# A decoder layer with experts on one core: another order of the step, routing in PSUM, and set-up loads counted in four groups

## The reference

```
x = x + self_attention(layernorm(x))             # 16 heads of 8, rope, causal
x = x + cross_attention(layernorm(x), ctx)       # 16 heads of 8, 77 keys
xn = layernorm(x)
p = softmax(xn @ router_w)                       # 8 ways; top1 picks one
shared = (xn @ sup * silu(xn @ sgate)) @ sdown   # hidden 512
routed = expert[top1](xn)                        # 7 experts, hidden 512; way 7 has none
x = x + 2 * p[top1] * routed + shared
```

## Time and profile before

| what | value |
|---|---|
| times of three runs | 1065.08, 1065.98, 1068.63 us; median 1065.98 |
| span of the profiled execution | 1065.7 us (that execution has no other time beside it) |
| start of the batch loop's first project_qkv | 26.1 us |
| last project_qkv, last shared_down, first expert matmul | 776.6, 842.62, 856.95 us |
| PE, DVE, ACT, POOL busy over the span | 93%, 82%, 69%, 59% |
| mean granted TensorE clock | 0.990 of full |

### The profile page before, as it was taken

How to read it: one execution, slowest core, us unless ns; L and a number is a source line. 1 busy time by engine, 2 the same in 40 slices (tenths; PEclk the granted TensorE clock), 3 DMA queues, 4 the chain that set the end, 5 groups by cost and what they waited for, 6 DMA issues and landing times.

```text
span 1065.7 us, 45022 instructions
## 1 busy us (share of the span) xinstructions
PE 992.5 (93%) x16200; PEld 818.3 (77%) x16201; DVE 870.9 (82%) x2853; ACT 737.2 (69%) x1557; POOL 631.4 (59%) x1488
## 2 busy tenths in 40 slices
PE   1579999999999999999999999999999999999995
PEld 1357777777777777777777777777777889999995
DVE  4367999999999999999999999999986457777774
ACT  0267878888888878888888888887875145555552
POOL 0346677777777677777777777767764124444443
PEclk9999999999999999999999999999999899999998
DMA  6222011000100010000100010000000122222220
GB/s 133 71 72 77 28 32 32 26 30 26 32 26 30 25 29 28 26 30 26 32 26 30 26 29 28 30 25 28 28 29 21 58 70 70 73 71 68 70 65 5
DMA packets 66648, 44.27 MB, mean 42 GB/s; under 512 B 24135, under 2 KB 61451, under 8 KB 66592
## 3 DMA queue, kind: packets, MB, share of 16 engines
q1 hardware_dynamic: 55424, 30.35, 10.5%
q0 software_dynamic: 5312, 12.18, 3.3%
q10 hardware_dynamic: 5856, 0.99, 0.7%
HBM read 23.96 MB, written 18.29 MB: 40 GB/s over the span
## 4 chain that ended last, share of the span: by engine, by line
PE 76%; DVE 10%; issue 4%; SPq 3%; DMA 2%; ACT 1%; POOL 1%; ACTq 1%; DVEq 0%; POOLq 0%
PE pv L1122 11%; PE scores L1302 6%; PE scores L1307 6%; PE ro L1318 6%; PE ro L1177 6%; PE scores L1163 5%; PE st L1232 5%; DVE arena L641 4%; PE scores L999 4%; PE scores L1169 4%; PE ro L1139 3%; PE pj L1145 3%; PE ro L1131 3%; PE ro L1150 2%; PE scores L1033 2%
## 5 line engine op out<-in xcount | busy, mean ns | idle before, releaser
L919 ACT ACTIVATE arena<-scores 128x1024 f32<-128x1024 f32 (+1 forms) x256 | 262.6, 1026 | 48.5 <-PE scores L1016 33.6
L641 DVE TENSOR_REDUCE arena<-scores 128x8 f16<-128x1024 f32 (+1 forms) x256 | 256.7, 1003 | 47.5 <-PE scores L1007 37.6
L859 ACT ACTIVATE arena<-st 128x128 f16<-128x128 f16 (+2 forms) x256 | 154.9, 605 | 7.9 <-PE st L1232 6.8
L859 ACT ACTIVATE arena<-arena 128x512 f16<-128x512 f32 (+2 forms) x192 | 92.9, 484 | 70.3 <-POOL arena L453 50.3
L1122 PE MATMUL pv<-arena 128*32 128x128 f32 (+1 forms) x4096 | 139.3, 277 | 0.0
L1122 PEld LDWEIGHTS pv<-arena 128*32 128x32 f32 (+1 forms) x4096 | 104.6, 110 | 17.1 <-issue 10.1
L439 POOL TENSOR_TENSOR arena<-arena,neg_half 128x1 f32<-128x1 f32 x192 | 106.5, 555 | 15.0
L449 POOL TENSOR_TENSOR arena<-arena 128x256 f32<-128x256 f32 x64 | 46.4, 725 | 78.9 <-DVE arena L633 78.9
L526 POOL DMA_INDIRECT out_dram<-x_tile x70 | 69.9, 998 | 38.5 <-POOL carried L525 26.1
L477 POOL TENSOR_TENSOR arena<-arena 128x128 f32<-128x128 f32 x128 | 51.7, 404 | 61.2 <-DVE arena L651 61.2
L1232 PE MATMUL st<-id,arena 128*128 128x128 f16 (+1 forms) x1024 | 74.0, 215 | 8.5 <-POOL arena L462 8.5
(11 more groups left out here) (175 smaller groups left out, 2681.3 us busy)
## 6 DMA issues: line engine op xcount, KB each, us to landing
x_tile<-xs SPq DMA_DIRECT2D x70, 129.0 KB, 2.0
arena<-arena SPq DMA_DIRECT2D x512, 4.0 KB
arena<-in_x_dram SPq DMA_DIRECT2D x64, 64.0 KB, 1.8
out_dram<-pay SPq DMA_DIRECT2D x64, 64.0 KB, 1.6
arena<-in_ctx_dram SPq DMA_DIRECT2D x64, 38.5 KB
w_gate<-in_L_ffn_gate_w_dram SPq DMA_DIRECT2D x7, 256.0 KB, 2.8
w_up<-in_L_ffn_up_w_dram SPq DMA_DIRECT2D x7, 256.0 KB, 3.1
w_down<-in_L_ffn_down_w_dram SPq DMA_DIRECT2D x7, 256.0 KB, 4.0
```

Source lines behind the costliest of these rows:

```text
L641: v.tensor_reduce(nmax[:, n, :].rearrange("p (m r s) -> p r m s", r=2, s=SLOT)[:, u, :, 0:HG], pair(s)[:, :, 0:HG * keys].rearrange("p m ( ...
L859: return a.activation(to, of, ACT.Copy)
L919: a.activation(e32[0:rows, 2 * n + u, :], scores[0:rows, 1024 * s:1024 * (s + 1)], ACT.Exp).then_inc(sexp_done[n][u], 1)
```

## The change

It does six things. (1) Every engine's step gets another order and other lags: PE now from 0 (`xT1_of`) to 10 (`router`, `shared_gate`, `shared_up`, `positions`, `shared_down`), DVE 0 to 10, POOL and ACT 0 to 9. (2) The pieces are put on other banks: gate and the positions on pv, up and down on st, stacks and both `values` on ro; the two pairs of `scores` hold scores alone. (3) Routing reads its logits in PSUM and writes its marks there; `logits_copy` and the identity matmul go, and `run_of` adds the base in a double buffer `run_pos`. (4) The variance plus eps and the negated mean move from POOL to DVE; the four `carry` go. (5) The loads count four semaphores, part of them go from ACT's queue to SP's, the set-up of cross attention runs inside steps 1 and 2, and a tanh loads ACT's table early. (6) The set-up's temporaries lie in the tile buffers instead of the loop's. The expert weights are still issued from step 3 on.

```diff
-        W_SELF = 16 * 10
-        W_ALL = 16 * 23
+        W_SELF = 16 * 5
+        W_ALL = 16 * 17
...
+            act.wait_ge(setup_z, 1)
+            a.activation(tanh_s[:, 0, 0:1], empty[:, 0:1], ACT.Tanh)
...
-            def logits_copy(b, p):
-                v.tensor_copy(logits[:, p, :], ro[:, 3 * P:3 * P + E]).then_inc(logits_ready, 1)
+            def top_of(b, p):
+                wait(dve, logits_psum, b + 1)
+                v.tensor_reduce(top[:, p:p + 1], pj[:, 0:E], axis=AX.X, op=ALU.min).then_inc(top_ready, 1)
             def marks_of(b, p):
-                v.scalar_tensor_tensor(out=mark[:, :], in0=logits[:, p, :], scalar=top[:, p:p + 1], in1=marks,
+                v.scalar_tensor_tensor(out=pj[:, E:2 * E], in0=pj[:, 0:E], scalar=top[:, p:p + 1], in1=marks,
                                        op0=ALU.is_equal, op1=ALU.mult).then_inc(marked, 1)
...
             def run_of(b, p):
-                v.tensor_copy(run_base[:, :], ro[:, 2 * P + E:2 * P + 2 * E]).then_inc(run_ready, 1)
+                v.tensor_tensor(run_pos[:, p, :].rearrange("p (n e) -> p n e", n=2), run_pos[:, 1 - p, E:2 * E].unsqueeze(1).to_broadcast([P, 2, E]),
+                                pv[:, 0:2 * E].rearrange("p (n e) -> p n e", n=2), ALU.add).then_inc(run_ready, 1)
+            def hot_pos_of(b, p):
+                v.scalar_tensor_tensor(out=hot_pos[:, :], in0=run_pos[:, p, 0:E], scalar=1.0, in1=hot16[:, p, :],
...
+            def ln1_var_of(b, p):
+                v.tensor_scalar_add(varp[:, 0:1], mv[:, 0, p, 1:2], EPS).then_inc(ln_var[0], 1)
...
+            nm0_turns = (((sh_hid, -7),), ((k2_ready, -3), (val2_ready, -3),), ((q2_ready, -3),), ((sh_added, -8),), ((nmT_ready[0], 0),),)
+            def self_max_turned(b, p):
+                turn(pe, b, *nm0_turns)
...
             def step(i, p):
+                at(i, p, 10, router)
+                at(i, p, 6, project_q2)
+                at(i, p, 10, shared_gate)
+                early(i, 10, busy_gate)
+                at(i, p, 6, project_kv2)
+                late(i, 6, busy_kv2)
+                at(i, p, 7, cross_max_turned)
+                two_turns(i, p, self_max, 2, 1, 0, sm1_turns, self_exp, 3, 0, 1, se0_turns)
+                at(i, p, 8, cross_values)
+                at(i, p, 10, positions)
+                at(i, p, 1, project_qkv)
+                late(i, 1, busy_qkv)
+                two_turns(i, p, self_exp, 3, 1, 0, se1_turns, self_max, 2, 0, 1, sm0_turns)
+                at(i, p, 6, stacks2)
+                at(i, p, 5, xT2_of)
+                at(i, p, 10, shared_up)
+                at(i, p, 3, self_values)
+                at(i, p, 2, self_max_turned)
+                at(i, p, 4, project_self_out)
+                two_turns(i, p, cross_exp, 7, 1, 0, ce1_turns, cross_max, 6, 0, 1, cm0_turns)
+                at(i, p, 8, project_cross_out)
+                at(i, p, 9, xT3_of)
+                at(i, p, 5, ctxT_of)
+                at(i, p, 10, shared_down)
+                early(i, 10, busy_down)
+                at(i, p, 0, xT1_of)
+                two_turns(i, p, cross_max, 6, 1, 1, cm1_turns, cross_exp, 7, 0, 0, ce0_turns)
+                at(i, p, 1, stacks)
```

More of the change, by code:

```diff
@@ L772, in _ @@
+                at(i, p, 9, hidden_of)
+            run(dve, step, 10)
             links = [0]
@@ L1110, in two_turns, with stack4 @@
                         round2(s2, u2, p2, g)
-            def values(b, p, n, *users):
-                vals, rows = ((val, P), (val2, C))[n]
-                wait(pe, sexp_done[n][0], b + 1)
-                wait(pe, sexp_done[n][1], b + 1)
-                turn(pe, b, *users)
+            def stack4(bank, to, src, rows, step):
+                for g in range(HG):
+                    last = t.transpose(bank[:, to + g * step:to + g * step + rows], src[0:rows, g * P:(g + 1) * P],
+                                       id16[0:rows, 0:rows])
+                return last
@@ new lines, in project_qkv, with project_kv2 @@
+            def project_qkv(b, p):
+                if isinstance(b, int) and b == 0:
+                    pe.wait_ge(setup_v, 3)
+                turn(pe, b, *qkv_turns)
+                t.matmul(pj[:, 0:3 * D], xnT[:, 0, :], w_qkv[:, :], start=True, stop=True).then_inc(qkv_psum, 1)
+            kv2_turns = (((q2_ready, 1),), ((sh_added, -4),), ((nmT_ready[0], 4),), ((sh_hid, -4),), ((k2_ready, 0), (val2_ready, 0),),)
+            def project_kv2(b, p):
+                if isinstance(b, int) and b == 0:
+                    pe.wait_ge(w_in, W_ALL)
+                turn(pe, b, *kv2_turns)
+                wait(pe, ctxT_ready, b + 1)
+                t.matmul(st[0:C, 0:2 * D], ctxT[:, 0:C], wc_kv[:, :], start=True, stop=True).then_inc(kv2_psum, 1)
@@ L1200, in busy_pj, with over @@
[L1200 removed]
+                    t.matmul(st[:, 0:D], w_qkv[:, 0:P], w_qkv[:, 0:P], start=c == 0, stop=c == FC - 1)
+            def over(b, users):
                 if all(b + user[0][1] > NB for user in users):
@@ L1220, in ctxT_of @@
-            def ctxT_of(b, p, *users):
-                turn(pe, b, *users)
-                wait(pe, ctx_in_s[p], 8 * b + 16 - 8 * p)
-                t.transpose(pj[:, 3 * D:3 * D + C], ctx_t[0:C, p, :], id32[0:C, 0:C]).then_inc(ctxT_psum, 1)
-            def project_kv2(b, p, *users):
-                turn(pe, b, *users)
-                wait(pe, ctxT_ready, b + 1)
-                t.matmul(pj[0:C, 0:2 * D], ctxT[:, 0:C], wc_kv[:, :], start=True, stop=True).then_inc(kv2_psum, 1)
-            def stack4(to, src, rows, step):
-                for g in range(HG):
-                    last = t.transpose(st16[:, to + g * step:to + g * step + rows], src[0:rows, g * P:(g + 1) * P],
-                                       id16[0:rows, 0:rows])
-                return last
```

892 lines of the change are left out of this document (503 added, 389 removed).

## The result

The changed kernel takes 992.5 us (median of 4 runs, 990.88 to 995.68) against 1066.35 for the kernel before; the ratio is 0.9317, 95% interval 0.9293 to 0.934. The forecast was 1028, range 1006 to 1058. The profiled execution spans 993.9 us.

| stage | before | after | change | forecast |
|---|---|---|---|---|
| start to first project_qkv | 26.11 | 12.38 | -13.7 | -15 |
| nine steps of the fill | 105.14 | 93.10 | -12.0 | -23 |
| 54 steady steps | 645.4 (11.951 each) | 580.3 (10.746 each) | -65.1 | -19 |
| batch 63's project_qkv to its shared_down | 66.0 | 84.6 | +18.6 | +18 |
| from there to the end | 223.1 | 223.5 | +0.4 | 0 |

A forecast was written before the change was run, and what follows sets the result against it. The prediction took a closed chain through both PE and DVE to bound the step. Steps -19, fill -23, set-up -15 and drain +18 gave -39 from 1065.7, so 1026.7, set at 1028 us; range 1006 to 1058.

The forecast's parts named there:

- VectorE's work, "about 10.9 us": Steady step: DVE's work after removals of 0.67 us and additions of 0.53, from 11.06 to about 10.9 us.
- the closed chain of 11.47 us: Steady step: self_max_turned through PE to shared_down, add_shared, DVE to hidden_of and back, 2.76 + 8.65 + 0.06 us.
- the forecast's step 11.6: Steady step: 11.6 us, between 11.35 and 11.96, because three chains lie near each other; -19 us over 54 steps.
- PE's work, "about 11.1 us a step": Steady step: without the identity matmul's 0.24 us all other PE pieces stay, needing about 11.1 us.
- PE alone is the bound: Rival for steady step and drain: PE's 11.3 us sets the step, drain at its load, kernel 1003 us; chance 0.12.
- The hold by POOL: Routing on DVE: marks_of and hot_of are held until POOL's instruction ends; PSUM inputs remove 0.29 + 0.20 us, 0.3 showing.
- Set-up: Start to first project_qkv: earlier first reduce and rope bias moved behind, start at 11 instead of 26.1 us, -15.
- Drain: After the last projection: lags to 10, PE's pieces 69.3 us plus 1 a step, 85 us; +18, bounds +9 and +27.
- Fill: First nine steps: a chain through rope, stacks and row maximum sets them, 82 instead of 105.1 us; -23, bounds -33 and -5.
- The slower rival: Steady loop: POOL holds five small SBUF operations on DVE, 1.25 us a step, about 67 us, kernel 1095; chance 0.09.

## Why the prediction was wrong, and where it was right

- **VectorE's work, "about 10.9 us", and with it the closed chain of 11.47 us**: the first step that failed, and the one that made the forecast's step 11.6. VectorE is busy 552.97/54 = 10.24 us a step, and from add_shared to hidden_of's end it needs 7.92 us where the chain had 8.65. I had taken over the old order's gaps between small operations that need each other's result, though the new order puts independent ones between; the sum has no term for that. The kernel with the dependent ones adjacent shows it: the same stretch is 8.71 us there (364.72 to 373.43), the step 11.461 and the kernel 1031.6, close to the forecast's 1028.
- **PE's work, "about 11.1 us a step"**: the second. TensorE needs at most 10.75, and with 11.1 as floor no shorter chain could have given the measured step. As 11.3 it was the rival "PE alone is the bound", which had the right mechanism, a size 0.55 too large and a chance of 0.12. I took distances between starts in the old step as streaming. Against the old trace project_kv2 goes from 0.69 to 0.43 on average, the three fp32 transposes from 0.63 to 0.45, the cross pairs from 0.83 to 0.70, while project_qkv grows from 0.65 to 0.82: those distances held waits.
- **The hold by POOL**: marks_of at 0.234 and hot_of at 0.226 us came as forecast (0.26, 0.2). For hot_of PSUM is a reason, as forecast (0.466 from SBUF at the same place); marks_of lost its hold by its new place, as the kernel with the routing in SBUF shows.
- **Set-up**: 12.4 us for 11, mostly by the counts, as forecast.
- **Drain**: +18.6 for +18. The number came, but that TensorE's load sets it isn't shown: without its unused products the profiled drain was not shorter, at a lower clock.
- **Fill**, 93.1 for 82: 4.5 is the clock, for which the forecast had nothing beyond the first two steps. Of the other 6.6, some 2.8 are the third to sixth step, 9.2 to 9.5 us instead of 8.6, where the row maxima's DMAs were left out of the chain; 3.6 are the last three, 10.5 to 10.7 instead of 8.6, 9.3 and 10.3.
- **The slower rival** falls: the four new one-column operations lie inside POOL's scatter in nearly all steps and take 0.14 us. Line 798 (hot_pos), at 0.159 us, has no instruction of POOL beside it in any of the 54 steps, so whether it would be held was not tested.

```profile
L776 DVE SCALAR_TENSOR_TENSOR pj<-pj,top,consts 128x8 f32<-128x8 f32 x54 | 12.6, 234 | 0.0
L785 DVE TENSOR_SCALAR hot<-pj,mark_top 128x8 f16<-128x8 f32 x54 | 12.2, 226 | 0.0
...
L798 DVE SCALAR_TENSOR_TENSOR hot_pos<-run_pos,hot 128x8 f32<-128x8 f32 x54 | 8.6, 159 | 0.0
```

The Trainium skill's rule on two SBUF inputs beside GpSimd (GPSIMD Engine Reference, section Specifications) speaks of that rival's line 798, which has two SBUF inputs; since POOL stands still beside it, no run here tests the rule on it.

## What to carry to other kernels

An engine's work can't be read from starts in a schedule that still has waits: put a spare instruction on each engine, at more than one place, and the engine whose spare costs its full price everywhere is the bound. On VectorE, put an independent operation between a small one and the one that needs its result; six such pairs were worth 0.7 us of an 11 us step here, and only 0.13 where TensorE's order left other waits. A wait of a weight load need not be a wait of TensorE: look in the chain of waits whether matmuls stream beside it.

## What the hardware showed that was not expected

A dependent neighbour on VectorE starts 0.17 to 0.27 us after a small predecessor, an independent one 0.05 to 0.14, with PSUM operands as with SBUF ones. An fp32 product of 128 columns added to TensorE costs 0.22 us, one of four left out of shared_down saves 0.08, with a wait for another engine right behind it. The same instructions in the fill took 88.6 us at full clock and 93.1 with a mean granted clock of 0.91 up to 40 us and 0.85 from there to 70 us.
